# A convolution kernel whose second block starts and ends differently: half-image first taps, factors spread by TensorE, energies shared between ScalarE and VectorE

## The chip, the cores and the metric

The kernel runs on one core of one Trainium2 chip. The metric is the device time of one execution in microseconds (us), from start to end of the program; lower is better.

## What is computed

The input `x` is (8, 64, 64, 64) in float32: 8 images, 64 channels, 64 x 64 pixels. The reference, cut to what matters:

```python
# block one: four scans, each over 64 lines: down, up, right, left
new = cur + relu(conv1d(prev, K))            # 64 -> 64 channels, 9 taps
# block two, per image of x (the result of block one)
pooled = x.mean((2, 3))
hdn = layernorm(pooled @ w_fc1.T) * ln1_w + ln1_b
dyn = hdn @ w_fc2.T                          # 25 taps per image and channel
out = depthwise_conv5x5(x, dyn)              # padding 2
out = layernorm over the channels of out, * ln2_w + ln2_b
out = gelu(einsum('bchw,oc->bohw', out, w_expand))       # 64 -> 256 channels
gx = sqrt(sum over h, w of out**2)           # one energy per image and channel
nx = gx / (gx.mean(over the 256 channels) + EPS)
out = gamma * (out * nx) + beta + out
out = einsum('bohw,co->bchw', out, w_shrink) + x         # 256 -> 64 channels
```

The factor `nx` needs the whole image, so nothing of an image can be shrunk before all its 4096 pixels have passed the GELU.

## The kernel before, in words

`build` runs `scans` (block one) and then `block_two`; the change touches `block_two` alone. Partition = channel and parity of the row (64 channels x 2 parities = 128), free = image, half row index, column.

Block two cuts the 8 images into `UNITS` = 16 units of half an image (16 row pairs x 64 columns = 1024 elements a partition). A unit has two chunks of 512 columns, which is one PSUM bank. A unit `u` passes these steps:

- `convolve` (TensorE, L1074): five of the 25 taps (those of the same row pair), as products with diagonal matrices `dyn_hi`, `dyn_lo`, in three parts each for precision, so 15 matmuls a chunk, into PSUM banks 0 to 3. The diagonals of image 0 are made on VectorE (`make_dyn`, L896), those of later images on GpSimd.
- `take_tap` (VectorE, L911): eleven taps, each `acc = src * weight + acc` on the PSUM sum in place; the last writes `inner`.
- `product` (ScalarE, L798) and `add_product` (GpSimd, L731): the other four taps, summed in `part`; `add_inner` (GpSimd, L744) adds them to `inner`.
- `square` (ScalarE, L804), `statistics` (TensorE, L1089: means over channels of `inner` and of its square), `square_mean` (ScalarE, L809), `make_var` (VectorE, L919, L921), `root` (ScalarE, L815), `make_rstd` (VectorE, L928). The result `rstd` is 128 partitions x 128 pixels: one factor a pixel, no longer one a channel.
- `spread_rstd` (SyncE's DMA queue): `rstd` is written to DRAM (L696), awaited, and read back with a broadcast to all partitions, as `rstd_wide` (two DMAs, L703). `norm` (GpSimd, L762) multiplies `inner` by it into `normed`.
- `expand` (TensorE, L1108): four a unit (2 halves of the 256 channels x 2 chunks), each into two banks; `gelu` (ScalarE, L827) reads them into `wide`; `add_squares` (ScalarE, L837, two a unit) squares `wide` with an accumulated sum, the energies.
- once an image: `sum_energy` (VectorE, L932), `root_energy` (ScalarE, L821), `respond` (TensorE, L1117, then five small VectorE steps L937 to L947, which scale the weights as `shrink_now`).
- `shrink` (TensorE, L1130: 4 matmuls a chunk, two records each in the trace), `finish` (VectorE, L956: adds bias and `x`), `store` (SyncE, L689: two DMAs of 256 KB a unit, once both chunks are finished).

Order. Every engine has its order written out by hand: a loop over slots `SLOTS_RUN` = -1 to 20, in which slot `s` convolves unit `s + 1`, takes the taps of `s`, does the statistics of `s - 1`, expands `s - 2`, sums squares of `s - 3` and shrinks and finishes `s - 5`. Slots 16 to 20 have no convolutions and taps left and drain the pipeline. An engine does its list in order; a wait holds all that is behind it. `expand` has one set of banks (4, 5) as long as convolutions run, and afterwards three (`exp_set`, `EXP_SETS`); `shrink` has one bank until the last image, then four (`out_bank`). In front of the slots stands the chain that makes the taps: VectorE `pooled` (L960), TensorE's first layer (L1043), VectorE's layer norm with ScalarE's square root (L964 to L975, L849), TensorE (L1045, L1051), VectorE (L985 to L997). TensorE's products of weights with weights (L1033 to L1040) and ScalarE's copies of them (L844 to L846) stand ahead of the step that they share an engine with.

The two waits ahead of ScalarE's square root in that chain are, in the code:

```python
act.wait_ge(pads, 1)      # L847
act.wait_ge(hid_var, 1)   # L848
act.activation(hid_stat[:, 2:3], hid_stat[:, 1:2], ACT.Sqrt, ...)   # L849
```

In the compiled program the first of the two is carried by the square root itself; the second is an instruction of its own, and the load of the square root's table (ACT_TABLE_LOAD) stands behind it.

## Time and profile before

| | us |
|---|---|
| median of 3 runs | 870.92 |
| lowest and highest of them | 868.53, 871.47 |
| the profiled execution, its own time | 868.42 |
| its span in the profile | 866.5 |
| block one, from the start to | about 502 |
| block two's taps (VectorE L911), from and to | 524.1, 815.3 |
| last `finish` ends | 861.5 |

Over the span TensorE is busy 90%, VectorE 70%, GpSimd 53% and ScalarE 48%, but these are averages over stages. From 524 to 815 us VectorE takes 11 taps a unit almost without a pause, and a unit costs some 17 to 19 us. Ahead of it lies a chain of small steps (502 to 524 us), behind it the drain (815 to 866 us); the change lies in these two stretches. In the rows a time is counted from the start of the span. A timeline row says when a group starts, how long it is busy, what it does, how many instructions (records) it has, and in brackets how long the engine was idle before it and what ended that.

### The profile page before, as it was taken

The numbers are of one execution on the slowest core, as the hardware profiler recorded it, in microseconds if no ns is written. First come the engines' busy times: TensorE is split into PE (matmuls) and PEld (weight loads), VectorE is DVE, ScalarE is ACT, GpSimd is POOL, SyncE is SP. The second block draws the span as 40 slices with busy tenths as digits, with TensorE's granted clock in tenths as the row PEclk, the third lists the DMA queues.
The fourth block names the chain that finished last, engine by engine and source line by source line (L and its number), as shares of the span: only waits on it lengthen the run. The fifth ranks groups of instructions, "written<-read, shape, count | busy, mean of one in ns | idle before, by whom it ended". The sixth has DMA issues, their size and how long they took to land. (4 is left out here: it accounts for less than half of the span.)

```text
span 866.5 us, 15588 instructions
## 1 busy us (share of the span) xinstructions
PE 782.7 (90%) x5383; PEld 635.1 (73%) x5383; DVE 610.1 (70%) x1111; ACT 413.7 (48%) x501; POOL 455.5 (53%) x443
## 2 busy tenths in 40 slices
PE   5999999999999999999999956778998999998675
PEld 5999999999999999999999945444444444444221
DVE  3666666666656666668888857887989899898712
ACT  5690004776770000000000033499999999989761
POOL 2333333333323333338888826797678787866610
PEclk9999999999999999999999968899999999999987
DMA  6660000000000000000000010222334333433233
GB/s 143 164 155 0 0 0 2 0 0 0 0 1 1 0 0 0 0 1 1 0 0 0 0 48 23 51 55 68 82 77 99 76 79 76 100 97 78 52 76 74
DMA packets 62195, 36.40 MB, mean 42 GB/s; under 512 B 41488, under 2 KB 60112, under 8 KB 62160
## 3 DMA queue, kind: packets, MB, share of 16 engines
q1 hardware_dynamic: 62160, 35.95, 17.6%
q8 instruction: 20, 0.33, 0.2%
q14 instruction: 15, 0.12, 0.0%
HBM read 18.37 MB, written 9.44 MB: 32 GB/s over the span
## 5 line engine op out<-in xcount | busy, mean ns | idle before, releaser
L481 PE MATMUL psum<-line_hi,taps_hi 128*128 128x256 f32 x1270 | 203.0, 292 | 11.9 <-DVE taps_lo L377 8.6
L495 PE MATMUL psum<-line_lo,taps_hi 128*128 128x256 f32 x1270 | 202.7, 291 | 0.8 <-DVE line_lo L430 0.8
L489 PE MATMUL psum<-line_hi,taps_lo 128*128 128x256 f32 x1270 | 202.5, 291 | 0.0
L430 DVE SCALAR_TENSOR_TENSOR line_lo<-psum,rest 128x256 fp32r<-128x256 f32 x254 | 108.1, 426 | 124.3 <-POOL rest L262 114.3
L481 PEld LDWEIGHTS psum<-line_hi,taps_hi 128*128 128x128 f32 x1270 | 177.1, 192 | 13.1 <-issue 9.4
L495 PEld LDWEIGHTS psum<-line_lo,taps_hi 128*128 128x128 f32 x1270 | 176.7, 192 | 2.0 <-DVE line_lo L430 1.8
L489 PEld LDWEIGHTS psum<-line_hi,taps_lo 128*128 128x128 f32 x1270 | 177.1, 192 | 0.0
L262 POOL TENSOR_TENSOR rest<-x,line_hi 128x256 f32<-128x256 f32 x127 | 82.8, 652 | 169.2 <-DVE line_hi L421 169.2
L314 ACT ACTIVATE by_h<-x (+1 forms) x128 | 85.7, 669 | 106.9 <-DVE x L410 105.3
L262 POOL TENSOR_TENSOR rest<-by_h,line_hi 128x256 f32<-128x256 f32 x127 | 91.6, 722 | 83.4 <-DVE line_hi L421 83.4
L731 POOL TENSOR_TENSOR part<-part,prod 128x960 f32<-128x960 f32 (+2 forms) x48 | 108.6, 2263 | 20.4 <-ACT prod L798 15.8
L911 DVE SCALAR_TENSOR_TENSOR psum<-x,tap_all,psum 128x930 f32<-128x930 f32 (+3 forms) x96 | 116.5, 1213 | 1.7
L410 DVE TENSOR_TENSOR x<-line_hi,line_lo 128x256 f32 (+1 forms) x190 | 105.4, 555 | 0.2
L1108 PE MATMUL psum<-normed,expand_w 64*128 64x512 f32 x256 | 73.8, 658 | 20.3 <-ACT wide L827 14.5
L911 DVE SCALAR_TENSOR_TENSOR psum<-crossed,tap_cross,psum 128x992 f32<-128x992 f32 (+1 forms) x64 | 80.8, 1262 | 11.0 <-PE psum L1074 9.6
L1074 PE MATMUL psum<-x_hi,dyn_hi 128*128 128x512 f32 x160 | 69.4, 434 | 17.5 <-DVE inner L911 14.2
L827 ACT ACTIVATE wide<-psum,expand_bias 128x1024 f32<-128x1024 f32 x64 | 70.5, 1106 | 20.6 <-PE psum L1108 20.4
L785 ACT ACTIVATE x_hi<-x 128x1024 fp32r<-128x1024 f32 x16 | 16.8, 1055 | 128.2 <-PEq L105 121.7
L744 POOL TENSOR_TENSOR inner<-inner,part 128x1024 f32<-128x1024 f32 x16 | 38.0, 2376 | 70.0 <-DVE inner L911 70.0
L421 DVE SCALAR_TENSOR_TENSOR line_hi<-psum,x 128x256 fp32r<-128x256 f32 x127 | 53.9, 425 | 21.9 <-PE psum L481 8.6
L1130 PE MATMUL psum<-wide,shrink_now 128*64 128x512 f32 x256 | 67.1, 653 | 2.1 <-DVE shrink_now L947 1.2
L1074 PE MATMUL psum<-x_lo,dyn_hi 128*128 128x512 f32 x160 | 67.6, 423 | 0.0
(126 smaller groups left out, 829.4 us busy)
## 6 DMA issues: line engine op xcount, KB each, us to landing
stage<-in_x_dram SPq DMA_DIRECT2D x32, 256.0 KB, 4.0
rstd_wide<-rstd_dram SPq DMA_DIRECT2D x32, 256.0 KB, 5.4
out_dram<-x SPq DMA_DIRECT2D x32, 256.0 KB, 5.4
crossed<-x SPq DMA_DIRECT2D x16, 256.0 KB, 3.6
crossed<-x SPq DMA_DIRECT2D x16, 240.0 KB, 3.6
rstd_dram<-rstd SPq DMA_DIRECT2D x16, 64.0 KB, 1.5
fc_in<-in_L_conv_w_fc_dram SPq DMA_DIRECT2D x2, 100.0 KB
taps<-in_L_conv_k_td_dram SPq DMA_DIRECT2D x2, 80.0 KB, 3.3
```

Source lines behind the costliest of these rows:

```text
L262: pool.tensor_tensor(rest[:, slot % 2, :].rearrange("p (b i) -> p b i", b=B), x_line, line_hi[:, (slot + 1) % SLOTS, :, REACH:REACH + WP]. ...
L314: act.activation(dst, src, ACT.Copy).then_inc(turned, 1)
L410: dve.tensor_tensor(kept_line(s, row_of(s, k)), line_hi[:, made, :, part].bitcast(F32), line_lo[:, made, :, part].bitcast(F32), ALU.add).t ...
L430: dve.scalar_tensor_tensor(out=line_lo[:, (slot + 1) % SLOTS, :, part], in0=as_lines(line_ps[slot][:, 0:LINE]), scalar=0.0, in1=as_lines(r ...
L481: mm = pe.matmul(line_ps[slot][:, 0:LINE], taps_hi[:, s, d, :], line_hi[:, slot, :, d:d + WP], start=(d == 0), stop=(d == OFFSETS - 1))
L489: pe.matmul(line_ps[slot][:, 0:LINE], taps_lo[:, s, d, :], line_hi[:, slot, :, d:d + WP], start=False, stop=False, skip_group_check=True)
L495: mm = pe.matmul(line_ps[slot][:, 0:LINE], taps_hi[:, s, d, :], line_lo[:, slot, :, d:d + WP], start=False, stop=(d == OFFSETS - 1), skip_ ...
L731: pool.tensor_tensor(dst, dst, other, ALU.add).then_inc(part_step, 1)
L827: act.activation(wide[:, m, :, u % WIDE, c * COLS:(c + 1) * COLS], exp_set(4 * u + 2 * m + c), ACT.Gelu, bias=expand_bias[:, m:m + 1]).the ...
L911: dve.scalar_tensor_tensor(out=dst, in0=src, scalar=weight, in1=here, op0=ALU.mult, op1=ALU.add).then_inc(tap_step, 1)
L1074: mm = pe.matmul(conv_ps[:, 2 * (u % 2) + c, :], weight[:, b % 2, n, :, :].rearrange("p o c -> p (o c)"), image[:, u % 2, CROWS * c:CROWS ...
L1108: mm = pe.matmul(exp_set(e)[:, hp, :], expand_w[half, m, :], normed[half, u % 2, c * COLS:(c + 1) * COLS], start=True, stop=True)
```

## The change

What it does, in four parts.

1. Head. TensorE's first layer (L1043) is put ahead of the products of weights. ScalarE's wait for `pads` is put ahead of the copies of the weights. `dyn_hi` of image 0 gets a semaphore of its own (`dyn_first`), so that the first two convolution matmuls need not wait for `dyn_lo`. VectorE takes unit 0's eleven taps in two passes: `first_chunk` on the upper 8 row pairs as soon as the first chunk is convolved, and then `take_tap` on the lower 8.
2. Factors of the last unit. In place of the way over DRAM, GpSimd makes one-hot matrices `spread` (`make_spread`, two copies of 512 elements a partition, from the identity), TensorE multiplies them with `rstd` (`widen`, 4 products of 128 x 128 x 128 a chunk, into banks 2 and 3), and VectorE multiplies `inner` by the result, a chunk at a time (`norm(c)`).
3. The drain's order. The slots end at 15, and the rest is a list for each engine. Unit 15's four expansions follow each other, without shrinks between them, and use two sets of banks. Of the last two units' four `add_squares`, ScalarE keeps one and VectorE gets three (`tensor_tensor_reduce`, 2048 elements a partition each).
4. Output. From unit 12 on, shrinks use more banks. Units 14 and 15 are stored by chunk: two DMAs of 128 KB each time.

The diff, cut to its core:

```diff
-        EXP_SETS = 3
-        FREE_CONV = 4 * (UNITS - 2)
+        EXP_SETS = 2
+        LAST = UNITS - 1
+        FREE_CONV = 4 * (LAST - 1)
...
-        SLOTS_RUN = range(-1, UNITS + 5)
+        SLOTS_RUN = range(-1, UNITS)
...
-            first = 4 if e < FREE_CONV else (4, 0, 2)[(e - FREE_CONV) % EXP_SETS]
+            first = 4 if e < FREE_CONV else (4, 0)[(e - FREE_CONV) % EXP_SETS]
...
         def out_bank(k):
-            return out_ps if k < 4 * (B - 1) else psum[:, 4 + k % 4, :]
+
+            if k < 2 * (LAST - 3):
+                return out_ps
+            return psum[:, (6, 7, 6, 7, 4, 5, 0, 1)[k - 2 * (LAST - 3)], :]
...
+            for u in range(LAST - 4, LAST - 1):
+                store(u)
+            for u in range(LAST - 1, UNITS):
+                for c in range(2):
+                    store_chunk(u, c)
+            sp.wait_ge(stored, 32 * (UNITS + 2))
...
+            def make_spread():
+
+                pool.wait_ge(part_step, PART_STEPS * UNITS)
+                for k in range(SUBS):
+                    row = kept["ident"][:, :].rearrange("p (g h k a) -> p g h k a", g=4, k=SUBS, a=1)[:, :, 0:2, k, :]
+                    pool.tensor_copy(spread[:, :, k, :].rearrange("p g (h c) -> p g h c", c=C),
+                                     row.to_broadcast([P, 4, 2, C])).then_inc(spread_made, 1)
...
+            make_spread()
+            add_inner(LAST)
+            norm(LAST - 1)
...
+            act.wait_ge(pads, 1)
             act.wait_ge(weights_mm, 1)
...
-            act.wait_ge(pads, 1)
             act.wait_ge(hid_var, 1)
...
+            add_squares(LAST - 2, 1)
+            square(LAST)
+            square_mean(LAST)
+            root(LAST)
+            root_energy(B - 2)
+            for i in range(4):
+                gelu(LAST - 1, i // 2, i % 2)
+                if i == 1:
+                    add_squares(LAST - 1, 0)
+            for i in range(4):
+                gelu(LAST, i // 2, i % 2)
+            root_energy(B - 1)
...
-                for t, full in ((tap_hi, dyn_hi), (tap_lo, dyn_lo)):
+                for t, full, ready in ((tap_hi, dyn_hi, dyn_first), (tap_lo, dyn_lo, dyn_ready)):
...
+                if u == 0:
+                    src, rows = src[:, CROWS - rows.start:rows.stop - rows.start, :], slice(CROWS, rows.stop)
...
+            def first_chunk():
+
+                dve.wait_ge(conv_done, 1)
+                dve.wait_ge(crossed_loaded[0], 32)
+                for i in range(N_DVE):
+                    src, rows, cols, weight = place(0, *DVE_TAPS[i])
+                    here = slice(rows.start, CROWS)
+                    dst = inner[:, 0, here, :] if i == N_DVE - 1 else acc[:, 0, here, cols]
+                    link(dve.scalar_tensor_tensor(out=dst, in0=src[:, 0:CROWS - rows.start, :], scalar=weight,
+                                                  in1=acc[:, 0, here, cols], op0=ALU.mult, op1=ALU.add))
...
+            def norm(c):
+                dve.wait_ge(wide_done, c + 1)
+                dve.tensor_tensor(normed[:, LAST % 2, c * COLS:(c + 1) * COLS],
+                                  inner[:, LAST % INNERS, c * CROWS:(c + 1) * CROWS, :].rearrange("p j w -> p (j w)"),
+                                  psum[:, 2 + c, :], ALU.mult).then_inc(normed_ready, 1)
+
+            def add_squares(u, m):
+                dve.wait_ge(gelu_done, 4 * u + 2 * (m + 1))
+                dve.wait_ge(energy_ready, 2 * u + m)
+                dve.wait_ge(energy_summed, B - 1)
+                grown = wide[:, m, :, u % WIDE, :]
+                dve.tensor_tensor_reduce(dump[:, :].rearrange("p (a n) -> p a n", a=2), grown, grown, 1.0, 0.0,
+                                         ALU.mult, ALU.add, energy[:, m, u % 2:u % 2 + 1]).then_inc(energy_ready, 1)
...
+            finish(LAST - 4, 0)
+            sum_energy(B - 2)
+            make_var(LAST)
+            make_rstd(LAST)
+            finish(LAST - 4, 1)
+            respond(B - 2)
+            norm(0)
+            norm(1)
+            finish(LAST - 3, 0)
+            add_squares(LAST - 1, 1)
+            finish(LAST - 3, 1)
+            add_squares(LAST, 0)
+            finish(LAST - 2, 0)
+            add_squares(LAST, 1)
+            sum_energy(B - 1)
+            respond(B - 1)
+            finish(LAST - 2, 1)
+            for u in (LAST - 1, LAST):
+                for c in range(2):
+                    finish(u, c)
...
         @block.tensor
         def _(pe):
+            pe.wait_ge(pooled_ready, 1)
+            pe.matmul(out_ps[0:B, 0:CR], pooled[:, :], kept["fc1_t"][:, :], start=True, stop=True).then_inc(pool_mm, 1)
...
+                    if (u, c, n, part) == (0, 0, 0, 2):
+                        pe.wait_ge(dyn_ready, 1)
...
+            def widen(c):
+                if c == 0:
+                    pe.wait_ge(rstd_ready, UNITS)
+                    pe.wait_ge(spread_made, SUBS)
+                    pe.wait_ge(tap_step, N_DVE * UNITS)
+                for g in range(2):
+                    for k in range(SUBS):
+                        at = (g * SUBS + k) * STAT_COLS
+                        mm = pe.matmul(psum[:, 2 + c, at:at + STAT_COLS], spread[:, 2 * c + g, k, :], rstd[:, LAST % 2, :],
+                                       start=True, stop=True)
+                mm.then_inc(wide_done, 1)
...
+            shrink(LAST - 4, 0)
+            statistics(LAST)
+            expand(LAST - 1, 0, 0)
+            expand(LAST - 1, 0, 1)
+            shrink(LAST - 4, 1)
+            respond(B - 2)
+            widen(0)
+            widen(1)
+            expand(LAST - 1, 1, 0)
+            shrink(LAST - 3, 0)
+            expand(LAST - 1, 1, 1)
+            shrink(LAST - 3, 1)
+            for m in range(HALVES):
+                for c in range(2):
+                    expand(LAST, m, c)
+            shrink(LAST - 2, 0)
+            shrink(LAST - 2, 1)
+            respond(B - 1)
+            for u in (LAST - 1, LAST):
+                for c in range(2):
+                    shrink(u, c)
```

## Rows read from the trace of the kernel before

**Rows 1.** Waits in the drain, 814 to 867 us: who <- whom: total, times, longest.

```profile
POOL normed L762 <- DMA rstd_wide<-rstd_dram: 11.0, 1, 11.0
```

**Rows 2.** Timeline of ScalarE (ACT) in the drain: start, busy, what, records, idle before.

```profile
823.74 2.12 ACT L827 ACTIVATE wide<-psum,expand_bias 128x1024 f32<-128x1024 f32 x2
825.88 1.91 ACT L837 ACTIVATE dump<-wide 128x2048 bf16<-128x2048 f32 x1
...
847.52 1.28 ACT L821 ACT_TABLE_LOAD   x1
```

**Rows 3.** Timeline of VectorE (DVE) in the drain.

```profile
822.36 0.95 DVE L928 RECIPROCAL rstd<-std 128x128 f32<-128x128 f32 x1 [1.10 <-ACT std L815]
...
849.83 0.16 DVE L937 TENSOR_SCALAR resp<-psum 128x1 f32<-128x1 f32 x1 [1.48 <-PE psum L1117]
...
860.74 0.75 DVE L956 SCALAR_TENSOR_TENSOR x<-psum,out_bias,x 128x512 f32<-128x512 f32 x1 [0.97 <-PE psum L1130]
```

**Rows 4.** Timeline of TensorE (PE) in the drain.

```profile
821.26 1.94 PE L1130 MATMUL psum<-wide,shrink_now 128*64 128x512 f32 x8
823.13 1.13 PE L1108 MATMUL psum<-normed,expand_w 64*128 64x512 f32 x4
824.19 0.60 PE L1117 MATMUL psum<-resp,mean_ce 128*128 128x1 f32 x4
...
849.07 0.72 PE L1117 MATMUL psum<-resp,mean_ce 128*128 128x1 f32 x4 [2.43 <-ACT resp L821]
851.03 9.66 PE L1130 MATMUL psum<-wide,shrink_now 128*64 128x512 f32 x32 [1.23 <-DVE shrink_now L947]
```

**Rows 5.** Durations and sizes on VectorE, 500 to 867 us (by form): busy, mean ns.

```profile
L956 DVE SCALAR_TENSOR_TENSOR x<-psum,out_bias,x 128x512 f32<-128x512 f32 x32 | 23.8, 745 | 28.9 <-PE psum L1130 28.9
...
L888 DVE TENSOR_TENSOR x_lo<-x,x_hi 128x1024 fp32r<-128x1024 f32 x2 | 2.4, 1212 | 0.0
```

**Rows 6.** Timeline of GpSimd (POOL) around its last work on unit 15.

```profile
815.43 2.35 POOL L744 TENSOR_TENSOR inner<-inner,part 128x1024 f32<-128x1024 f32 x1 [4.39 <-DVE inner L911]
```

**Rows 7.** Stretches of 2 us: PE, PEld, DVE, ACT, POOL busy, granted clock, DMA share, GB/s.

```profile
800.00:802.00 2.00, 0.00 (x0) 0.00 (x0) 1.97 (x3) 1.37 (x3) 2.00 (x2) 1.00 0.00 0
...
850.00:852.00 2.00, 0.97 (x4) 0.36 (x6) 0.85 (x4) 0.00 (x0) 0.00 (x0) 0.50 0.95 200
```

**Rows 8.** The output's DMAs from 850 us on: time from issue to landing.

```profile
L689 SPq DMA_DIRECT2D out_dram<-x x4: 595/600/677, 858.1 to 862.5; - x4
...
DMA to landing us min/median/max: 3.3/3.5/3.9
```

**Rows 9.** Timeline of TensorE in the head.

```profile
503.65 0.68 PE L1033 MATMUL psum<-expand_t,centre 128*128 128x128 f32 x4 [2.80 <-PEq L105]
...
505.40 0.22 PE L1043 MATMUL psum<-fc_t,pooled 128*8 128x16 f32 x2
...
515.33 0.77 PE L1074 MATMUL psum<-x_hi,dyn_hi 128*128 128x512 f32 x1 [3.35 <-DVE dyn_lo L896]
...
516.32 0.63 PE L1074 MATMUL psum<-x_hi,dyn_lo 128*128 128x512 f32 x1
...
520.08 0.39 PE L1074 MATMUL psum<-x_hi,dyn_lo 128*128 128x512 f32 x1
...
538.21 0.80 PE L1074 MATMUL psum<-x_hi,dyn_hi 128*128 128x512 f32 x1 [7.00 <-DVE inner L911]
```

**Rows 10.** Timeline of VectorE in the head.

```profile
503.65 0.42 DVE L960 TENSOR_REDUCE pooled<-line_sum 128x8 f32<-128x256 f32 x1 [1.28 <-PEq L105]
...
505.73 0.16 DVE L964 TENSOR_REDUCE hid_stat<-psum 8x1 f32<-8x16 f32 x1 [1.43 <-PE psum L1043]
...
514.36 0.82 DVE L896 TENSOR_TENSOR dyn_lo<-ident_half,tap_lo 128x640 fp32r<-128x640 f32 x1
...
524.08 5.17 DVE L911 SCALAR_TENSOR_TENSOR psum<-crossed,tap_cross,psum 128x992 f32<-128x992 f32 x4 [8.62 <-PE psum L1074]
```

**Rows 11.** Timeline of ScalarE in the head.

```profile
506.61 1.28 ACT L849 ACT_TABLE_LOAD   x1 [0.58 <-DVE hid_stat L967]
```

More of the change, by code:

```diff
@@ L615, in block_two @@
         xlo_ready = sem("xlo_ready")
+        dyn_first = sem("dyn_first")
         dyn_ready = sem("dyn_ready")
@@ L689, in store, with store_chunk @@
                     sp.dma_start(o[b, p][:, j:j + ROWS, :], x[C * p:C * p + C, b, j:j + ROWS, :]).then_inc(stored, 16)
+            def store_chunk(u, c):
+                b, j = u // 2, ROWS * (u % 2) + CROWS * c
+                sp.wait_ge(finished, 2 * u + c + 1)
+                for p in range(2):
+                    sp.dma_start(o[b, p][:, j:j + CROWS, :], x[C * p:C * p + C, b, j:j + CROWS, :]).then_inc(stored, 16)
             def spread_rstd(u):
@@ L765, in _ @@
             pool.wait_ge(dyn_ready, 1)
-            for s in range(UNITS + 2):
+            def make_spread():
[4 more added lines that the diff above has]
+                                     row.to_broadcast([P, 4, 2, C])).then_inc(spread_made, 1)
+            for s in range(UNITS):
                 w, e = s - 1, s - 2
-                if w in range(UNITS):
+                if w >= 0:
                     add_inner(w)
@@ L771, in _ @@
                     norm(e)
-                if s < UNITS:
-                    for n in range(1, N_ACT):
-                        add_product(s, n)
+                for n in range(1, N_ACT):
+                    add_product(s, n)
                 if s + 2 < UNITS:
@@ L998, in _ @@
             dve.sem_inc(taps_known, 1)
+            first_chunk()
             for s in SLOTS_RUN:
@@ L1041, in _ @@
             mm.then_inc(weights_mm, 1)
-            pe.wait_ge(pooled_ready, 1)
-            pe.matmul(out_ps[0:B, 0:CR], pooled[:, :], kept["fc1_t"][:, :], start=True, stop=True).then_inc(pool_mm, 1)
             pe.wait_ge(hid_ready, 1)
@@ L1066, in convolve @@
                         pe.wait_ge(xlo_first, u + 1)
-                    if u % 2 == 0:
+                    if u == 0:
+                        pe.wait_ge(dyn_first, 1)
+                    elif u % 2 == 0:
                         pe.wait_ge(dyn_ready, b + 1)
```

27 lines of the change are left out of this document (16 added, 11 removed).

## The prediction

> **What bounds the kernel now.** I read the forty slices first (TensorE, VectorE and ScalarE share the middle, and both ends of block two show holes), then the waits and the timelines of the two ends. What takes measurable time out of this kernel has to come from there, because the slots from 538 to 815 us keep their instructions.
>
> *Head.* VectorE runs a chain of small steps up to `dyn_lo`, whose end at 515.18 releases TensorE's first convolution at 515.33 [rows 9, 10]. Its first chunk ends at 520.47 (520.08 + 0.39), but VectorE stands idle until 524.08, when both chunks are done [rows 9, 10]. The reader is to see TensorE's 7.00 us of idle time ahead of 538.21, ended by VectorE's last tap of unit 0 [rows 9]: from 524 to 538 everybody waits for these eleven taps. So what the taps gain, all later work gains.
>
> *Drain.* VectorE has unit 15's `rstd` at 823.31 (822.36 + 0.95) [rows 3]. Then GpSimd waits 11.0 us for the factors' way over DRAM, the longest wait of the drain [rows 1], and four expansions, four GELUs and two sums of squares follow. The last sum of squares ends just ahead of 847.52, then come a table load, the response, and 32 shrink records from 851.03 to 860.69; the last finish ends at 861.49 [rows 2, 3, 4], and the last store takes the span to 866.5.
>
> **The change, part by part.** All times are on the clock of before; the head's shift is added at the end. A change of 0.3%, 2.6 us, is about what a measurement of this kernel can tell from none.
>
> *Head, order.* `pooled` is ready at 504.07 [rows 10]. With the first layer first, its product starts there instead of at 505.40, 1.3 us earlier. But ScalarE's square root stays behind the copies of the weights, and those wait for weight products that now start at 504.4 and take the same 1.75 us (503.65 to 505.40) [rows 9]: to 506.15. ScalarE's copies ended at 506.03 (0.58 before 506.61) [rows 11], 0.63 after that point; now at 506.8. The moved wait for `pads` lets the table load start at once, where it waited for `hid_var` until 506.61. Load from 506.8 to 508.05, against 507.89: 0.15 us later. The two edits cancel; bounds: 0.5 earlier and 0.5 later (TensorE's clock could fall during the weight products).
>
> *Head, `dyn_first`.* Two of three products use `dyn_hi`, ready 0.82 us before `dyn_lo`. The first matmul starts at 514.6; the third is due 0.99 us later (515.33 to 516.32) [rows 9], after `dyn_lo`. The whole stream gains 0.75 us. Bounds 0 and 0.8.
>
> *Head, two passes.* VectorE starts at 520.5 - 0.75 + 0.15 = 519.9. Eleven full taps cost 1.29 us each (5.17 for four), 14.1 in all [rows 10]. The halves have the same elements and 11 fixed costs more. A 512-element instruction takes 0.745 us [rows 5], so a fixed cost is near 0.21, plus 0.04 for the step from one to the next: 11 x 0.25 = 2.75, together 16.8 us. End 536.7 in place of 538.15. **Head: 1.45 us gained**, bounds 0.5 and 1.9. Nobody else was due before 538, so it is passed on.
>
> *Factors.* Gone are three DMAs and their waits, and GpSimd's norm of unit 15 (2.35 us by its like in [rows 6]). The copies that make the one-hot matrices (two of 512 elements; half of a 2.35 us instruction each, at most) fall into GpSimd's 4.39 us of idle time ahead of 815.43 [rows 6]: nothing; without this cover they would cost 2.4 us ahead of the norm of unit 14. TensorE's new list: second expansion of unit 14 from 821.26 to 822.3 (an expansion is 1.06, a shrink 1.87 from start to start [rows 4]), shrink to 824.2, response 0.6 to 824.8. `widen` is 8 fp32 products, 16 records. The nearest rows are the products of weights, of the same shape among them: 0.11 each for sixteen, 0.17 for the first four [rows 9]. I take 0.13, between them: 2.1 us, bounds 1.75 and 2.7, ending 826.9. VectorE's two norms of 512 elements (0.745 with PSUM as a source [rows 5]) end at 827.6, when unit 15's expansions could begin; before they began after the 11 us wait. TensorE's and ScalarE's own lists now come later than that.
>
> *The list after it.* Expansion to 828.0, shrink to 829.9, expansion to 830.9, shrink to 832.8 (`wide` has three places, so unit 15's GELU needs unit 12's shrinks). ScalarE has been free since 829.0, waits, and runs unit 14's last GELU to 832.0. Then unit 15: expansion 832.8 to 833.9, GELUs at 1.06 [rows 2], the third and the fourth held up by the two sets of banks by some 0.2 together: 838.4. ScalarE's table load follows at once, since nothing but GELUs is left: off the path.
>
> *Energies.* VectorE squares 2048 elements with a sum. No row of before has that at this size. Two-source work of 1024 elements takes 1.212 [rows 5]; twice that less one fixed cost is 2.3. The lower bound is ScalarE's 1.91 for the same work [rows 2], the upper one twice 2.3. I take 2.35, the rate of the engine that does it. Sums: 832.0 to 834.4; 836.1 to 838.5; then `finish` of unit 13 stands ahead of the third and waits for its shrink, which ends only at 839.2, behind the last expansion; the third sum runs from 839.95 to 842.3. That is the wait this order adds: 1.4 us. Reduction, square root (0.4), response 0.72 on TensorE, 1.2 us of small steps on VectorE (849.83 to 851.03) [rows 3, 4]: shrinks start at 844.65 instead of 851.03. **6.4 us gained.** The 32 shrink records keep their 9.66 us for now, the last finish ends at 855.1.
>
> *What the Trainium skill says of the energies.* The trace's VectorE takes two fp32 operands from SBUF at full rate [rows 5], but in an operation without a sum. The Trainium skill, Vector Engine (DVE) Microarchitecture Reference, section 7, says that a scalar-tensor-tensor instruction with two SBUF sources that are not bf16 runs at half rate, because no port is left for the accumulator. By that a sum would take some 4.5 us; no row of before shows it.
>
> *Stores.* Before, 5.0 us lay between the last finish and the end: two issues of 0.6 and a landing of 3.3 to 3.9 [rows 8]. Half the bytes: the issue perhaps 0.1 shorter each, the landing shorter by up to half. I take 1.2 us gained, bounds 0.4 and 1.9.
>
> **Sum:** 1.45 + 6.4 + 1.2 = 9.05. The profiled execution took 868.42 us, so 859.4 for its like. The median of the three runs lies 2.5 above it; from 870.92 I get **861.9 us**.
>
> **The rivals.**
> *Clock held.* In the last shrinks TensorE had half its clock (0.50 at 850 us) [rows 7], 1.2 GHz, after idle stretches of 2.43 and 1.23 us [rows 4]. After the change the idle stretches are 1.5 and 1.2 us, behind twenty dense microseconds, and at 800 to 802 us TensorE was wholly idle with its clock at 1.00 [rows 7]. If it stays at 2.4 GHz, each chunk's shrink takes 1.87 or less: four finish 2.65 us earlier, **859.2**.
> *Sums at half rate.* At 4.5 us each VectorE alone sets the pace: 832.0 + 3 x 4.5 + two finishes 1.5 = 847.0 in place of 842.3. The gain falls to 4.35, **866.6**. For it speaks that no such sum at length is in the trace, against it that plain two-source work is not slowed [rows 5]. This is the rule of the microarchitecture page of the Trainium skill cited above.
> *The taps' gain is not passed on.* If ScalarE or GpSimd sets the slots' pace before unit 2, the 1.45 is lost: 863.4. Against it: TensorE, with its 7.00 us wait, had long been ready [rows 9].
> *Slower.* One mechanism: VectorE's sums. They are in series on one engine, ahead of the only path to the end. At s us each their end is 832.0 + 1.5 + 3s; all 9.05 us are used up at s = 5.9, 2.9 ns an element against 1.2 in [rows 5]. At 7 us each the kernel would take 874. For it speaks only that the instruction is a custom one.
> *It doesn't do what it says:* if the response of image 7, not the factors' way, had been the bound, nothing would be gained; the 11.0 us wait [rows 1] stands in that very chain, so I leave this little.
>
> **How the numbers follow.** Forecast as summed 0.45 (861.9); clock held 0.30 (859.2); half rate 0.14 (866.6); gain of the taps lost 0.05 (863.4); no change 0.03; slower 0.03. Faster by over 0.3% are the first four: 0.94, of which I take 0.01 for surprises. The range takes in the half rate and, on the other side, the held clock with the better bounds of head and stores (another 1.1): 858.0 to 866.8. It leaves some 0.15 out.
>
> **What would show it.** In the profile after: first tap at 519.9 and unit 0's last tap ending at 536.7; no DMA of `rstd` for unit 15 and no long GpSimd wait; `widen` of some 2.1 us at 824 to 827; three sums of 2.35 us on VectorE; the response's matmuls 6.4 us earlier than 849.07, less the head; the granted clock in the last shrinks decides between forecast and first rival. Sums near 4.5 us, or a slot rhythm in which unit 1 does not start earlier, would prove me wrong.

## The result and the profile after

| | before | after |
|---|---|---|
| median of the runs | 870.33 us (868.53 to 871.47, 4 runs) | 860.15 us (859.75 to 860.41, 4 runs) |
| ratio, 95% interval | | 0.988 [0.987, 0.990] |
| profiled execution, its span | 868.42, 866.5 us | 859.75, 857.8 us |
| mean granted clock of TensorE | 0.969 | 0.974 |

The change takes 10.2 us off by the medians, 8.7 us in the two profiled spans. In the text below, "before" and "after" stand for the two kernels. I cut every trace at the same points: block two's start (VectorE's `pooled` reduction), the start of unit 0's first tap, the ends of the last tap of unit 0 and of unit 15, the last 32 shrink records, the last `finish`, and the span's end. All numbers are us. "Start" is block two's start from the start of the span. "First tap" and "unit 0" (the end of its last tap) are counted from block two's start. Each later column is a distance from the point before it: "middle" runs from the end of unit 0's last tap to the end of unit 15's, "shrinks" is the time of the last 32 shrink records, and "end" is what lies between the last `finish` and the end of the span. (Some 0.8 us, from the last shrink to the end of the last `finish`, is in no column.)

| kernel | start | first tap | unit 0 | middle | to last shrinks | shrinks | end | span |
|---|---|---|---|---|---|---|---|---|
| before | 503.65 | +20.43 | +34.50 | 277.14 | 35.74 | 9.66 | 5.01 | 866.5 |
| after | 503.13 | +18.25 | +35.16 | 277.22 | 28.99 | 8.78 | 3.72 | 857.8 |

The drain (the three columns ahead of the span) gave 35.74 + 9.66 + 5.01 - 28.99 - 8.78 - 3.72 = 8.9 us. The head, in this pair of traces, gave nothing: unit 0 ends 0.66 us later, counted from block two's start. Block two itself starts 0.52 us earlier in the trace of after; the change doesn't touch block one, and over all traces of this study that start lies anywhere from 502.1 to 505.0.

The chain of waits of after, from 840 us on (start, us, what):

```profile
839.89 2.28 DVE dump L998
...
842.21 0.17 DVE resp L1003
...
842.40 0.21 ACT resp L853
...
842.66 0.62 PE psum L1226 x4
...
844.15 0.30 DVE shrink_now L1018
...
844.50 8.81 PE psum L1241 x32
...
853.33 0.75 DVE x L1027
```

The reader is to see that no table load stands in it and that the third sum (L998) now leads to the response. TensorE's timeline in the drain of after shows the new list, from `widen` (L1199) on, against [rows 4]:

```profile
825.01 2.03 PE L1199 MATMUL psum<-rstd,prod 128*128 128x128 f32 x16
826.97 1.13 PE L1217 MATMUL psum<-normed,expand_w 64*128 64x512 f32 x4
...
832.83 1.99 PE L1217 MATMUL psum<-normed,expand_w 64*128 64x512 f32 x8
835.17 2.13 PE L1217 MATMUL psum<-normed,expand_w 64*128 64x512 f32 x8 [0.36 <-ACT wide L859]
837.23 3.65 PE L1241 MATMUL psum<-wide,shrink_now 128*64 128x512 f32 x16
842.66 0.60 PE L1226 MATMUL psum<-resp,mean_ce 128*128 128x1 f32 x4 [1.77 <-ACT resp L853]
844.50 8.78 PE L1241 MATMUL psum<-wide,shrink_now 128*64 128x512 f32 x32 [1.24 <-DVE shrink_now L1018]
```

VectorE's timeline of the same stretch, against [rows 3]:

```profile
826.38 1.39 DVE L989 TENSOR_TENSOR normed<-inner,psum 128x512 f32<-128x512 f32 x2
...
832.22 2.29 DVE L998 CUSTOM_DVE_ANT_1 dump<-wide 128x2048 bf16<-128x2048 f32 x1 [1.45 <-ACT wide L859]
...
836.15 2.29 DVE L998 CUSTOM_DVE_ANT_1 dump<-wide 128x2048 bf16<-128x2048 f32 x1 [0.96 <-ACT wide L859]
...
839.22 0.75 DVE L1027 SCALAR_TENSOR_TENSOR x<-psum,out_bias,x 128x512 f32<-128x512 f32 x1 [0.77 <-PE psum L1241]
839.89 2.28 DVE L998 CUSTOM_DVE_ANT_1 dump<-wide 128x2048 bf16<-128x2048 f32 x1
```

ScalarE's, against [rows 2], the last two GELUs and the table load behind them:

```profile
836.35 2.12 ACT L859 ACTIVATE wide<-psum,expand_bias 128x1024 f32<-128x1024 f32 x2 [0.23 <-PE psum L1217]
838.48 1.28 ACT L853 ACT_TABLE_LOAD   x1
```

Three sums of 2.29 us each, 2048 elements; the third waits from 838.45 to 839.89 for unit 13's `finish` (L1027). The stores of after, by the DMA issues (out<-in, count, KB, median us to landing), against [rows 8]:

```profile
out_dram<-x SPq DMA_DIRECT2D x28, 256.0 KB, 5.4
...
out_dram<-x SPq DMA_DIRECT2D x8, 128.0 KB, 2.5
```

TensorE's timeline in the head of after, against [rows 9]:

```profile
503.60 0.22 PE L1125 MATMUL psum<-fc_t,pooled 128*8 128x16 f32 x2 [3.27 <-DVE pooled L1031]
503.75 1.22 PE L1128 MATMUL psum<-expand_t,centre 128*128 128x128 f32 x4
...
505.85 0.60 PE L1134 MATMUL psum<-beta,shrink_t 128*64 128x1 f32 x8
...
515.08 0.77 PE L1171 MATMUL psum<-x_hi,dyn_hi 128*128 128x512 f32 x1 [2.61 <-DVE dyn_hi L941]
515.64 0.63 PE L1171 MATMUL psum<-x_lo,dyn_hi 128*128 128x512 f32 x1
...
520.34 0.55 PE L1171 MATMUL psum<-x_hi,dyn_hi 128*128 128x512 f32 x1
520.72 0.39 PE L1171 MATMUL psum<-x_lo,dyn_hi 128*128 128x512 f32 x1
520.95 0.39 PE L1171 MATMUL psum<-x_hi,dyn_lo 128*128 128x512 f32 x1
```

ScalarE's copies of those products, the table load behind them, and VectorE's first tap in the same trace, against [rows 11] and [rows 10]:

```profile
506.57 0.38 ACT L877 ACTIVATE expand_w<-psum 128x256 f32<-128x256 f32 x1 [1.45 <-PE psum L1134]
...
507.10 1.28 ACT L881 ACT_TABLE_LOAD   x1
```

```profile
521.38 3.08 DVE L968 SCALAR_TENSOR_TENSOR psum<-crossed,tap_cross,psum 128x496 f32<-128x496 f32 x4 [5.44 <-PE psum L1171]
```

The products of the weights run from 503.75 to 506.4, 2.65 us where before took 1.75. The convolution's matmuls come every 0.43 us up to 520.34 and every 0.23 us soon after. The granted clock says the same: 0.50 from 515 to 520 us, which is 1.2 GHz, and 1.00 from 522 on, 2.4 GHz. Before had its first chunk of 15 matmuls done in 5.14 us, after in 6.26 (515.08 to 521.34). That is where the head's gain went in this trace.

### The profile page after: what moved, and what is told of

It is laid out like the page before. It is cut to its first block and busy times, and to the rows that moved or that the text cites. A ratio compares the mean times of both kernels' runs of the same rounds, so it can differ in the third digit from the quotient of the medians.

```text
span 857.8 us, 15635 instructions
## 1 busy us (share of the span) xinstructions
PE 783.1 (91%) x5399; PEld 637.1 (74%) x5399; DVE 620.9 (72%) x1130; ACT 407.9 (48%) x495; POOL 454.5 (53%) x444
## 5 line engine op out<-in xcount | busy, mean ns | idle before, releaser
L753 POOL TENSOR_TENSOR part<-part,prod 128x960 f32<-128x960 f32 (+2 forms) x48 | 108.7, 2264 | 21.4 <-ACT prod L830 16.8
L957 DVE SCALAR_TENSOR_TENSOR psum<-x,tap_all,psum 128x992 f32<-128x992 f32 (+5 forms) x96 | 113.6, 1183 | 1.7
L957 DVE SCALAR_TENSOR_TENSOR psum<-crossed,tap_cross,psum 128x992 f32<-128x992 f32 (+3 forms) x64 | 78.7, 1230 | 2.5 <-PE psum L1171 1.0
L859 ACT ACTIVATE wide<-psum,expand_bias 128x1024 f32<-128x1024 f32 x64 | 70.5, 1107 | 17.8 <-PE psum L1217 17.6
L817 ACT ACTIVATE x_hi<-x 128x1024 fp32r<-128x1024 f32 x16 | 16.8, 1055 | 129.2 <-PEq L105 121.7
L1171 PE MATMUL psum<-x_hi,dyn_lo 128*128 128x512 f32 x160 | 67.3, 421 | 0.0
```

The costliest lines, as they stand in the source:

```text
L753: pool.tensor_tensor(dst, dst, other, ALU.add).then_inc(part_step, 1)
L859: act.activation(wide[:, m, :, u % WIDE, c * COLS:(c + 1) * COLS], exp_set(4 * u + 2 * m + c), ACT.Gelu, bias=expand_bias[:, m:m + 1]).the ...
L957: dve.scalar_tensor_tensor(out=dst, in0=src, scalar=weight, in1=here, op0=ALU.mult, op1=ALU.add).then_inc(tap_step, 1)
L1171: mm = pe.matmul(conv_ps[:, 2 * (u % 2) + c, :], weight[:, b % 2, n, :, :].rearrange("p o c -> p (o c)"), image[:, u % 2, CROWS * c:CROWS ...
```

## The experiments

Each has 4 to 12 runs, beside runs of the kernel before on the same chip, and the ratio is to those runs of before (medians 869.78 to 870.31). Differences to after's 860.15 compare medians of separate sessions. Medians of before differ by 0.5 us between the sessions, and each ratio's interval is some 1 to 1.7 us to either side, so a difference below about 2 us is not clear of noise by the medians alone. There the cut points carry the argument. The cut points of one profile each, in the columns above:

| kernel | median us | ratio, interval | first tap | unit 0 | middle | to last shrinks | shrinks | end |
|---|---|---|---|---|---|---|---|---|
| head_only | 868.59 | 0.998 [0.997, 0.999] | +18.24 | +35.14 | 277.22 | 35.12 | 8.79 | 5.00 |
| drain_only | 862.05 | 0.991 [0.989, 0.992] | +21.86 | +35.93 | 278.91 | 28.72 | 8.78 | 3.67 |
| one_pass | 861.00 | 0.991 [0.989, 0.993] | +21.34 | +35.40 | 278.92 | 28.70 | 8.79 | 3.69 |
| weights_first | 858.47 | 0.987 [0.985, 0.989] | +17.61 | +34.51 | 277.19 | 28.95 | 8.78 | 3.74 |
| sqrt_first | 859.59 | 0.988 [0.986, 0.990] | +15.38 | +32.28 | 279.18 | 28.74 | 8.78 | 3.74 |
| warm_head | 858.91 | 0.987 [0.985, 0.988] | +16.59 | +33.50 | 277.11 | 28.66 | 9.82 | 3.68 |
| over_dram | 864.84 | 0.993 [0.992, 0.995] | +17.97 | +34.86 | 279.83 | 32.50 | 8.79 | 3.59 |
| sums_on_act | 862.38 | 0.991 [0.989, 0.992] | +18.34 | +35.24 | 277.45 | 30.34 | 9.94 | 3.77 |
| late_finish | 857.49 | 0.985 [0.983, 0.987] | +18.34 | +35.24 | 277.44 | 27.81 | 7.09 | 3.68 |
| warm_gap | 858.82 | 0.987 [0.986, 0.989] | +18.26 | +35.16 | 277.13 | 28.90 | 7.09 | 3.75 |
| best1 | 855.26 | 0.983 [0.981, 0.985] | +15.42 | +32.32 | 279.24 | 27.42 | 7.09 | 3.68 |
| edits_joined | 853.89 | 0.982 [0.980, 0.984] | +16.17 | +33.08 | 278.82 | 27.42 | 7.09 | 3.71 |

**head_only** and **drain_only**: one end of the change each.

head_only is before with the four edits of the head, here against before; drain_only is after with the same four undone:

```diff
+            act.wait_ge(pads, 1)
             act.wait_ge(weights_mm, 1)
...
-            act.wait_ge(pads, 1)
             act.wait_ge(hid_var, 1)
...
+                    if (u, c, n, part) == (0, 0, 0, 2):
+                        pe.wait_ge(dyn_ready, 1)
...
+            first_chunk()
             for s in SLOTS_RUN:
...
+            pe.wait_ge(pooled_ready, 1)
+            pe.matmul(out_ps[0:B, 0:CR], pooled[:, :], kept["fc1_t"][:, :], start=True, stop=True).then_inc(pool_mm, 1)
```

> The kernel before with the edits of the head alone (first layer first, pads wait moved, dyn_first, first taps in two passes). Theory A: the head brings nothing, because TensorE's products of weights now run inside the chain at half clock and hold ScalarE's square root back by 1.0 us, which eats what the two other edits bring. Expected: from block two's start to the end of unit 0's last tap 35.2 us (34.5 before), ratio to before 0.999 to 1.001. Theory B: the head's forecast of 1.45 us was right and the profile of after only caught a bad phase of TensorE's clock. Expected: 33.1 us for that stretch, ratio 0.998.

> The changed kernel with the head of before. Theory A (the head is worth nothing): as fast as the changed kernel, ratio 0.988, 860.2 us. Theory B (the head is worth 1.45 us): 861.6 us, ratio 0.990.

head_only is worth 1.6 us (870.22 - 868.59), drain_only 8.2, together 9.8 of the 10.2, so within the noise the two ends add up. head_only met the stretch of its theory A (35.14 us, 35.2 expected) and the ratio of its theory B (0.998). The two don't contradict each other if the trace of before was a lucky one for the head, and drain_only shows that it was: with the same head instructions, its unit 0 ended at +35.93 where before had +34.50. The runs of before point the same way. Of the 17 beside head_only, 15 took 869.2 to 872.4 us at a mean granted clock of 0.961 to 0.964; the traced execution, 868.42 us at 0.969, is like the two others, 867.93 and 868.40 us at 0.967 and 0.969. drain_only's products of the weights:

```profile
502.69 1.19 PE L1112 MATMUL psum<-expand_t,centre 128*128 128x128 f32 x4 [2.80 <-PEq L105]
...
505.28 0.22 PE L1122 MATMUL psum<-fc_t,pooled 128*8 128x16 f32 x2
```

They take 2.6 us here and 1.75 in [rows 9], so the root comes 0.84 us later, and the first chunk takes 5.73 us instead of 5.14. Against this head, after's is 0.77 us shorter.

**one_pass** and **weights_first**: two parts of the head undone by themselves.

one_pass against after:

```diff
-            first_chunk()
             for s in SLOTS_RUN:
```

weights_first against after:

```diff
-            pe.wait_ge(pooled_ready, 1)
-            pe.matmul(out_ps[0:B, 0:CR], pooled[:, :], kept["fc1_t"][:, :], start=True, stop=True).then_inc(pool_mm, 1)
...
             mm.then_inc(weights_mm, 1)
+            pe.wait_ge(pooled_ready, 1)
+            pe.matmul(out_ps[0:B, 0:CR], pooled[:, :], kept["fc1_t"][:, :], start=True, stop=True).then_inc(pool_mm, 1)
```

> The changed kernel with unit 0's taps in one pass again, after both chunks. Theory A (the two passes gain the second chunk's matmuls, 3.6 us, and pay 2.8 us for eleven more fixed costs): unit 0's last tap 35.9 us after block two's start in place of 35.2, 860.9 us. Rival (the fixed costs eat it all): 35.2 us or less, 860.2 us or faster.

> The changed kernel with TensorE's first layer behind the products of weights again (ScalarE's wait for pads stays moved). Theory A (putting the first layer first does harm, because the square root stands behind the copies anyway and its table load now could start right behind them): the square root ends 4.9 us after block two's start in place of 5.5, 0.6 us earlier, 859.5 us. Rival (the reordering helps as meant): 0.5 to 1 us slower, 861 us.

By the medians the two passes are worth 0.85 us (861.00 - 860.15), which is within the noise. Their first tap starts 3.1 us earlier (+18.25 against +21.34), and the eleven taps then take 16.91 us where one pass takes 14.06. In the traces this leaves a gain of 0.24 us, between the 0.7 of theory A and nothing. The first layer's early start is a loss: with the weights' products ahead of it again, unit 0 ends 0.65 us earlier, as expected. The median falls by 1.7, more than the cut points account for (in its trace block two also starts 0.5 us earlier, which isn't the edit's). The square root stands behind ScalarE's copies of those products, so starting them late moves the root, whatever the first layer gains.

**sqrt_first**: ScalarE's square root (and its table load) ahead of the three copies. (Not ahead of the second `x_hi`, as the expectation says: only its wait for `pads` is.)

```diff
             split_high(0)
+            act.wait_ge(pads, 1)
             split_high(1)
-            act.wait_ge(pads, 1)
+            act.wait_ge(hid_var, 1)
+            act.activation(hid_stat[:, 2:3], hid_stat[:, 1:2], ACT.Sqrt, bias=eps_col[0:B, :],
+                           scale=1.0 / CR).then_inc(hid_sd, 1)
-            act.wait_ge(pads, 1)
             act.wait_ge(weights_mm, 1)
...
-            act.wait_ge(hid_var, 1)
-            act.activation(hid_stat[:, 2:3], hid_stat[:, 1:2], ACT.Sqrt, bias=eps_col[0:B, :],
-                           scale=1.0 / CR).then_inc(hid_sd, 1)
```

> The changed kernel with one move: ScalarE's square root of the layer norm stands ahead of its three copies of weights, and the second x_hi. Theory A: the copies are what held it, so the root starts at its table load's end, some 3.2 us after block two's start in place of 5.3, and all that follows comes 2.0 us earlier: 858.2 us. Theory B (the copies don't matter, the clock does): within 0.5 us of the changed kernel's 860.15.

The head did what was expected and more: the root starts 2.0 us earlier, the first chunk takes 5.35 us instead of 6.26, and unit 0 ends at +32.28, 2.9 us less. The time did not follow: 859.59, 0.6 us less, within the noise. The profile shows the middle longer by 2.0 us, half of it in units 1 to 5 and half in the last unit, and in the last unit a lower clock. The windows of 790 to 816 us (PE, PEld, DVE, ACT, POOL busy, granted clock, DMA share, GB/s) of before, after and sqrt_first:

```profile
790.00:816.00 26.00, 17.95 (x99) 7.60 (x101) 23.16 (x27) 20.71 (x22) 12.95 (x7) 0.99 0.34 83
```

```profile
790.00:816.00 26.00, 19.49 (x97) 7.71 (x99) 23.03 (x27) 19.91 (x21) 13.66 (x9) 0.90 0.37 84
```

```profile
790.00:816.00 26.00, 19.64 (x93) 7.59 (x93) 21.99 (x25) 19.19 (x20) 14.27 (x8) 0.81 0.34 80
```

The column before the last two is the granted clock: 0.99, 0.90, 0.81. The last unit took 16.1, 16.5 and 17.5 us in them. Between 615 and 790 us the clock is 1.00 in all three.

**warm_head**: 11 spare fp32 products (128 x 128, into a bank not in use) on TensorE, five behind the weights' products and six behind the products that make the taps, ahead of the first convolution.

```diff
             mm.then_inc(weights_mm, 1)
+            busy(5, 3)
...
             mm.then_inc(pool_mm, 1)
+            busy(6, 3)
```

> The changed kernel with 5 + 6 spare fp32 matmuls (128 columns, into a bank that is free there) put on TensorE behind the products of weights and ahead of the first convolution, where it stood idle. Theory A (the clock took the head's gain): the first chunk's 15 matmuls run at 2.4 GHz, 3.8 us in place of 6.3, and unit 0's last tap comes 2.3 us earlier after block two's start (32.9 in place of 35.2 us), 858 us. Rival: the spare matmuls delay the chain or the clock stays down, no gain or up to 1 us slower.

TensorE's timeline of warm_head:

```profile
512.22 2.93 PE L1126 MATMUL psum<-x,ident 128*128 128x128 f32 x12
514.90 0.77 PE L1178 MATMUL psum<-x_hi,dyn_hi 128*128 128x512 f32 x1
...
516.31 0.55 PE L1178 MATMUL psum<-x_hi,dyn_hi 128*128 128x512 f32 x1
516.70 0.41 PE L1178 MATMUL psum<-x_lo,dyn_hi 128*128 128x512 f32 x1
```

The clock rises at 516.3, with the fourth matmul, where after had it at 520.3, with the thirteenth. The first chunk takes 4.59 us instead of 6.26 and the first tap comes 1.66 us earlier; 2.3 us was expected, with the clock high from the first matmul. The median is 1.2 lower, and no run of warm_head is as slow as the fastest of after. What the clock's low level cost the first chunk is so shown by giving the engine work. In the same trace the last 32 shrinks took 9.82 us instead of after's 8.78, with the same drain instructions and the same idle stretches ahead of them:

```profile
840.37 0.61 PE L1233 MATMUL psum<-resp,mean_ce 128*128 128x1 f32 x4 [1.77 <-ACT resp L853]
842.21 9.82 PE L1248 MATMUL psum<-wide,shrink_now 128*64 128x512 f32 x32 [1.23 <-DVE shrink_now L1018]
```

So what a low clock costs the last shrinks differs by some 1 us from trace to trace.

**over_dram**: unit 15's factors by way of DRAM and GpSimd's norm again, all else as after.

> The changed kernel with the last unit's factors over DRAM again (write, read back, GpSimd's norm), all else as changed. In the trace of the changed kernel unit 15's first expansion starts at 832.8, behind unit 12's second shrink; over DRAM the norm would be done 10.2 us after rstd at 823.9, so at 834.1. Theory A (order, not the way, is the main part): 1.3 us later, 861.4 us. Theory B (the 11 us wait was the main part of the 6.5 us gained): 5 us later or more, 865 us.

```diff
+            spread_rstd(LAST)
             for u in range(LAST - 4, LAST - 1):
                 store(u)
...
-            make_spread()
             add_inner(LAST)
             norm(LAST - 1)
+            norm(LAST)
...
-            widen(0)
-            widen(1)
...
-            norm(0)
-            norm(1)
```

By the medians 4.7 us slower than after. Its trace is that of the slowest of its five runs (867.36 us): block two starts 1.9 us later in it and the middle is 2.6 longer, and nothing shows that either is the edit's. The edit's own part is the 3.5 us between the last tap and the last shrinks. TensorE's row of unit 15's first three expansions:

```profile
839.11 4.54 PE L1190 MATMUL psum<-normed,expand_w 64*128 64x512 f32 x12 [3.87 <-POOL normed L785]
```

and GpSimd's ahead of it:

```profile
835.29 3.77 POOL L785 TENSOR_TENSOR normed<-inner,rstd_wide 128x1024 f32<-128x1024 f32 x1 [10.72 <-DMA rstd_wide<-rstd_dram]
```

The wait for the way over DRAM is back, 10.72 us where [rows 1] has 11.0. From the last tap, the expansions of unit 15 start 2.06 us later than after's (19.38 us against 17.32), and the four of them then take 5.9 us instead of 4.5, behind TensorE's 3.87 us of idle time and at a granted clock of 0.59 and 0.56 between 839 and 843 us. So the time of theory B came out, but only 2.06 us of it is the later norm. Of the 8.2 us of the drain, 4.7 by the medians, or 3.5 by these traces, hang on the way of the factors. The order of the lists (unit 15's expansions in a row, two sets of banks) was taken away by no run, so its share is not shown apart.

**sums_on_act**: all four sums of unit 14 and 15 on ScalarE, as before.

```diff
-            for i in range(4):
-                gelu(LAST - 1, i // 2, i % 2)
-                if i == 1:
-                    add_squares(LAST - 1, 0)
-            for i in range(4):
-                gelu(LAST, i // 2, i % 2)
+            for u in (LAST - 1, LAST):
+                for i in range(4):
+                    gelu(u, i // 2, i % 2)
+                    if i % 2 == 1:
+                        add_squares(u, i // 2)
...
-            add_squares(LAST - 1, 1)
...
-            add_squares(LAST, 0)
...
-            add_squares(LAST, 1)
```

> The changed kernel with the three sums of squares of units 14 and 15 back on ScalarE, in their old places behind the GELUs. Theory A (the drain's gain comes from the order of TensorE's and ScalarE's lists; sharing the energies alone is worth little): ScalarE has 1.9 us gaps in which the first of the three fits, so the last sum ends at 842.2 against 842.1, and then the table load of 1.3 us is on the path: last shrinks 1.1 to 1.5 us later, 861.4 us. Theory B (as the prediction reads, the sums are a main part): three sums of 2.1 us in series, 5 us or more, 865 us.

By the medians 2.2 us slower than after. The last sum ends at 842.79 and the table load follows it, on the path again:

```profile
840.88 1.91 ACT L869 ACTIVATE dump<-wide 128x2048 bf16<-128x2048 f32 x1
...
842.90 1.28 ACT L853 ACT_TABLE_LOAD   x1
```

Counted from the last tap, the last sum ends at 26.8 us, against 26.7 in after: ScalarE's gaps hold the sums, as theory A says, and what costs is the table load. The shrinks start 1.35 us later, behind an idle stretch of 2.88 us, and take 9.94 instead of 8.78. That the longer stretch is the cause of the last 1.2 us isn't shown, since warm_head had 9.82 behind 1.77.

**late_finish**: the `finish` of unit 13's first chunk behind the last sum.

```diff
-            finish(LAST - 2, 0)
             add_squares(LAST, 1)
             sum_energy(B - 1)
+            finish(LAST - 2, 0)
             respond(B - 1)
```

> The changed kernel with VectorE's finish of unit 13's first chunk moved behind the last sum of squares and the reduction. If that finish is what delays the third sum (it starts 1.5 us after its data), the third sum starts at 838.5 and the last shrinks 1.4 us earlier: 858.8 us. Rival: TensorE's shrink of unit 13 and the clock set the end anyway: within 0.4 us of 860.15.

TensorE of late_finish:

```profile
841.80 0.60 PE L1226 MATMUL psum<-resp,mean_ce 128*128 128x1 f32 x4 [0.47 <-ACT resp L853]
843.64 7.09 PE L1241 MATMUL psum<-wide,shrink_now 128*64 128x512 f32 x32 [1.24 <-DVE shrink_now L1018]
```

By the medians 2.7 us less than after, twice what the wait was worth. The shrinks come 1.2 us earlier after the last tap. TensorE's idle stretch ahead of the response is 0.47 us instead of 1.77, and all 32 shrinks run at the full clock, 7.09 us for 8.78.

**warm_gap**: ten spare products in the gaps ahead of the last shrinks, six before the response and four behind it.

```diff
             shrink(LAST - 2, 1)
+            busy(6, 2)
             respond(B - 1)
+            busy(4, 2)
```

> The changed kernel with 6 + 4 spare fp32 matmuls (128 columns) on TensorE in the two idle stretches ahead of the last shrinks. Theory A (the clock falls in these stretches): the 32 shrink records take 7.1 us in place of 8.8, 858.5 us. Rival: the clock falls in spite of them, or they delay the response: 860 to 860.5 us.

The same two microseconds, 845 to 847, in after and in warm_gap (columns as above):

```profile
845.00:847.00 2.00, 2.00 (x8) 0.73 (x6) 0.11 (x1) 0.00 (x0) 0.00 (x0) 0.50 0.26 58
```

```profile
845.00:847.00 2.00, 2.00 (x12) 0.69 (x10) 0.75 (x1) 0.00 (x0) 0.00 (x0) 1.00 0.37 82
```

Clock 1.00 for 0.50, shrinks 7.09 us for 8.78. The median is 1.3 us less; the four runs, 857.84 to 861.05, overlap after's, so the trace and not the time carries this. So what after's last shrinks lost is the clock, and work in the gaps ahead of them keeps it. Over all fourteen traces this holds without exception: the four in which the stretch ahead of the response is short or filled (late_finish, warm_gap, best1, edits_joined) have 7.09, the ten others 8.78 to 9.94.

**best1** joins sqrt_first, late_finish, warm_gap's products (two and four) and seven spare 512-column products in the head. **edits_joined** leaves ScalarE's order alone and joins weights_first, warm_head, late_finish and warm_gap's products (two and four).

> All that the runs so far favour, together: square root ahead of the copies, finish of unit 13 behind the last sum, spare matmuls in the last gap (2 + 4, 128 columns, fp32), and in the head 2 + 5 spare matmuls of 512 columns (fp32r, x_hi by x_hi) in place of the short fp32 ones, which left the clock at 1.2 GHz until 516 us. Theory A (gains add up): head 2.9 + 1.7, drain 1.2 + 1.7, 7.5 us in all, 852.7 us. Rival (as in the run with the square root first, units 1 to 5 and the last unit give some 2 us back through TensorE's clock): 854.7 us.

> The kernel after with three edits together, the middle left alone: the products of the weights ahead of the root's (after took 35.16 us from block two's start to the end of unit 0; weights_first 34.51), 11 spare products in the head (warm_head 33.50), and the third unit-13 finish behind the last sum, with 6 spare products in the gap ahead of the last shrinks (late_finish: shrinks 27.81 us after the last tap, 7.09 us long; warm_gap 7.09). If the gains of the head add up and stay: u0 at +32.9, the middle 277.2 as in after and warm_head (not 279.2 as in sqrt_first and best1), shrinks at +27.4 for 7.09; sum 860.15 - 2.2 - 2.8 = 855.2, which is best1's time (855.26) by another route. If any shorter head is taken back by units 1 to 5 and the last unit, as sqrt_first's 2.9 us were (2.0 back): middle 279.2, time 857.2. If the middle stays and late_finish and warm_gap add beyond the shrinks' 7.09: 854.5 or less.

best1 took 855.26 us, near its rival's 854.7. Its spare products in the head brought nothing (first tap +15.42, sqrt_first +15.38), its middle is the long one (279.24), and its drain gave all it should (27.42 and 7.09). edits_joined came out at 853.89 us, 6.3 below after, and has the lowest median of the study; its profiled run is the slowest of its five, 855.93 (852.83 to 855.93). I had expected a middle of 277.2, and that trace shows 278.82, with a clock of 0.83 between 790 and 816. So the median fits the best of the three expectations (854.5 or less), while the trace has the long middle of the second.

## Why the prediction held, and where not

The forecast was 861.9 us, 858.0 to 866.8; the runs gave 860.15. Step by step:

- **Factors, list, energies: right, to 0.4 us.** The forecast was `widen` 2.1 us ending at 826.9, last GELU ended at 838.4, sums of 2.35, third from 839.95, shrinks at 844.65. The trace: 2.03 us, 827.0, 838.47, sums of 2.29, third from 839.89, shrinks at 844.50. From the last tap, 28.99 against 29.36. (One trace differs from another by as much: head_only, with before's drain, has 35.12 where before has 35.74.) The norms of 512 elements on VectorE took 0.69 each, and GpSimd's copies for the one-hot matrices stayed in its idle time (1.16 us for both; 3.62 us of it are left). That the sums moved to VectorE pay through the table load, and hardly through an earlier last sum, is what sums_on_act adds.
- **The wait that the order adds: right.** 1.4 us was forecast behind unit 13's `finish`; 839.89 - 838.45 is 1.44, and late_finish removed it. That it also costs the clock was not in the working.
- **Sums at half rate: refuted.** 2.29 us for 2048 elements is 1.1 ns an element, about the rate of the two-source work in [rows 5] (1.212 us for 1024). The rule of the Trainium skill, Vector Engine (DVE) Microarchitecture Reference, section 7, is for the scalar-tensor-tensor instruction; here the sum is done by another operation (CUSTOM_DVE_ANT_1 in the rows), and it isn't slowed. The slower rival, which needed more than 5.9 us a sum, falls with it.
- **Clock held: it was not.** The forecast kept 9.66 us, the rival took 2.65 off (four chunks at its own 1.87 would make 2.2). After has 8.78: the first chunk of the last shrinks runs at 1.2 GHz (845 to 847: 0.50), the last two at 2.4 (849 to 853: 1.00), and before's trace too has its last two `finish`es only 1.72 us apart. The 0.9 us less than before are not the change's: head_only has before's drain, idle stretches of 2.43 and 1.24 us, and 8.79. With one idle stretch shorter (late_finish) or both filled (warm_gap) the rival's case is there, 7.09, a gain of 2.57.
- **Stores: right.** 1.3 us gained against 1.2 forecast. About 1.0 of it is the landing, 2.5 us for 128 KB against 3.3 to 3.9 (median 3.5) for 256 KB; an issue is no cheaper, 0.6 us in both. All traces with the stores by chunk have 3.6 to 3.8 us in the last column, the two without 5.0.
- **Head: mis-sized in the profile, about right by the medians.** The step that failed is "the two edits cancel" and with it the first tap at 519.9. Counted from block two's start it should have come at +16.25; it came at +18.25. Of these 2.0 us, 0.87 are the root's chain (products of the weights at 1.2 GHz, 2.65 us instead of the 1.75 that I took from [rows 9]), and 1.1 are the first chunk, twelve of whose fifteen matmuls run at 1.2 GHz. I had named the first as a bound ("TensorE's clock could fall during the weight products") and priced it at 0.5; it is the usual case here: in the traces of all twelve experiments these products take between 2.3 and 2.7 us. The terms of the edits themselves held: `dyn_first` 0.74 us (the convolution starts behind `dyn_hi`; `dyn_lo`, on which it waited before, ends that much later), two passes 16.91 us against 16.8 forecast. By the medians the head is worth 1.6 us (head_only) or 1.9 (drain_only against after), where 1.45 was forecast.
- **From profile to median.** I added the 2.5 us between the profiled execution of before and its median. After's profile lies 0.4 below its median. The fast head of before's trace may be a part of that 2.5: it is 1.43 us shorter than drain_only's, which has the same instructions. On the spans the parts sum to 0.3 us slower than forecast: head +2.1, middle +0.1, block two's start -0.5, way to the last shrinks -0.4, shrinks -0.9, stores -0.1. That this sum is so small is luck: the head missed by 2.1, and 1.4 of it came back from block two's start and the last shrinks, neither of which the change shortened. On the medians the forecast was 1.75 too high. Of this, 0.6 is before's own median, 870.92 in three runs and 870.33 in four; the other 1.1 is a gain of 10.2 where 9.05 was forecast. The trace of before, whose head was not the usual one, would explain the sign, but no run shows the size.

**What stays open.** Why the middle takes 277.2 us in some traces and 278.8 to 279.2 in others. It follows neither the head's length (one_pass has 278.92 at +35.40, after 277.22 at +35.16) nor the drain's code. The granted clock between 790 and 816 us goes with the last unit's length in all fourteen traces: 16.1 us at 0.95 and 0.99, 16.5 at 0.88 to 0.91, 17.5 or 17.6 at 0.81 to 0.87. (A unit of before lasts 15.9 to 22.0 us; the 17 to 19 given ahead of the prediction holds for the mean alone.) Each kernel has one trace, so whether a kernel has a long middle always or by chance isn't settled. edits_joined's runs fall into two groups, 852.8 to 853.9 us at a mean granted clock of 0.977 to 0.978 and 855.8 to 855.9 at 0.973 to 0.974, with the traced one in the upper group, and that speaks for chance. For the same reason sqrt_first's lost 2 us are not shown to be caused by its edit.

## What to carry to other kernels

Read the price of a TensorE step that follows an idle stretch together with the granted clock of that stretch, and take the slow level as the case to expect; the one trace of before can have been lucky. Ahead of a final dense stretch, close the idle gaps first: here 1.3 us less of waiting brought 2.7 by the medians, since it kept the clock as well. And when a step is moved ahead, follow what the next engine has queued behind the step that it was moved past: in after the first layer came earlier and the root later.

## What the runs showed of the hardware that was not expected

- TensorE's granted clock stayed low while the engine was busy. In warm_head it was busy for 11.64 of the 13 us from 503 to 516, up to 514.9 with products of at most 128 columns and then with the convolution's 512, at a granted clock of 0.50. The clock rose at 516.3, during the convolution. The window (columns as above):

```profile
503.00:516.00 13.00, 11.64 (x53) 10.56 (x54) 7.67 (x25) 4.16 (x8) 0.34 (x5) 0.50 0.32 80
```

- In over_dram a GpSimd product of 1024 elements took 3.77 us (835.29 to 839.06) where its likes take 2.37. VectorE's two-source sum ran from 834.56 to 836.85 and its next instruction to 837.53, beside it. No run took one of the two away, so that VectorE's work is the cause isn't shown. The Trainium skill, GPSIMD Engine Reference, section 1, says that GpSimd's interface to SBUF is shared with VectorE and contended when VectorE reads two inputs from SBUF; by that rule, the trace agrees, 3.77 us for 2.37.
- VectorE's sum of squares of 2048 fp32 elements takes 2.29 us, ScalarE's 1.91 [rows 2]; on ScalarE it is faster and still the worse place, since ScalarE's next table load, 1.28 us, then stands behind the last sum and on the path (sums_on_act).
